# An adaLN transformer block with causal attention and a routed FFN: norms and route in pieces, value products of two units together

## The reference, cut to what matters

```python
mod = (silu(c) @ wmod).reshape(8, 6, 1, -1)      # sa, ca, ga, sb, cb, gb; |ga|, |gb| at least 0.25
h = layernorm(x) * (1 + ca) + sa
q, k, v = (lora_linear(h, ...) for 3 weights)     # x @ w.T + (x @ a.T @ b.T) / 16; 16 heads of 16
attn = softmax(where(causal, q @ k.T / 4, -inf))
x = x + ga * lora_linear(attn @ v, wo, ao, bo)
h = layernorm(x) * (1 + cb) + sb
w = top-2 of softmax(h @ Wg.T + bg), over 4 experts
base = h @ Wi.T                                   # 1024 wide
lora_e = (h @ A_e.T) @ B_e.T                      # per expert, rank 4
x = x + gb * sum_e w_e * (relu(base + lora_e) @ Wo.T)
```

## Time and profile before

| | us |
|---|---|
| median of 3 runs | 2129.84 (2129.48 to 2133.99) |
| profiled run, its own time | 2129.05 |
| its span | 2127.3 |
| TensorE busy | 1889.3 (89%), mean granted clock 0.957 |
| VectorE busy | 1219.6 (57%) |
| ScalarE busy | 943.9 (44%) |
| GpSimd busy | 489.7 (23%) |
| one full body (770.2 to 1022.8) | 252.6 |

### The profile page before, as it was taken

How to read it: one execution, slowest core, us unless ns; L and a number is a source line. 1 busy time by engine, 2 the same in 40 slices (tenths; PEclk the granted TensorE clock), 3 DMA queues, 4 the chain that set the end, 5 groups by cost and what they waited for, 6 DMA issues and landing times.

```text
span 2127.3 us, 31511 instructions
## 1 busy us (share of the span) xinstructions
PE 1889.3 (89%) x11124; PEld 978.3 (46%) x11124; DVE 1219.6 (57%) x2729; ACT 943.9 (44%) x1701; POOL 489.7 (23%) x791
## 2 busy tenths in 40 slices
PE   7699887999889997999979999799988999799858
PEld 5233443545335453454534454354533545343535
DVE  3767585555755566555665558555575555654142
ACT  2256553454444544444444444345444454444321
POOL 3122112222122312222122221222212231122213
PEclk9899998999899998999999999999989999899979
DMA  5413221212201122021211212121220112110100
GB/s 169 84 51 72 71 69 45 68 33 66 80 10 61 31 66 80 16 70 33 68 60 34 68 30 71 45 68 34 65 80 8 63 31 66 31 38 3 36 0 20
DMA packets 103024, 111.37 MB, mean 52 GB/s; under 512 B 20084, under 2 KB 96976, under 8 KB 102872
## 3 DMA queue, kind: packets, MB, share of 16 engines
q1 hardware_dynamic: 102856, 109.34, 18.1%
q10 hardware_dynamic: 16, 0.02, 0.0%
HBM read 75.20 MB, written 33.57 MB: 51 GB/s over the span
## 4 chain that ended last, share of the span: by engine, by line
PE 72%; DVE 14%; ACT 6%; issue 4%; SPq 2%; DMA 2%; POOL 1%; ACTq 0%; POOLq 0%; DVEq 0%
PE ov L768 11%; PE dense L848 11%; PE st L753 10%; PE mxs L739 10%; PE dense L859 5%; PE dense L825 5%; PE dense L783 5%; PE dense L833 4%; DVE negm L1139 3%; PE dense L724 3%; ACT probs L907 2%; PE mxs L743 2%; SPq L580 1%; PE dense L850 1%; DVE negm_left L1139 1%
## 5 line engine op out<-in xcount | busy, mean ns | idle before, releaser
L907 ACT ACTIVATE probs<-st 128x512 f32<-128x512 f32 (+1 forms) x1216 | 669.2, 575 | 653.8 <-PE st L753 644.1
L1139 DVE TENSOR_REDUCE negm<-mxs 128x1 f32<-128x384 f32 (+4 forms) x736 | 427.0, 615 | 212.7 <-PE mxs L743 209.6
L739 PE MATMUL mxs<-k_st,q_st 96*128 96x512 bf16 (+3 forms) x1536 | 469.7, 333 | 65.6 <-DVE negm L1139 59.4
L753 PE MATMUL st<-q_st,k_st 98*128 98x512 bf16 (+3 forms) x1536 | 452.8, 334 | 56.6 <-DMA q_st<-m_row 40.8
L1139 DVE TENSOR_REDUCE negm_left<-mxs 128x1 f32<-128x512 f32 x512 | 335.3, 685 | 139.8 <-PE mxs L739 138.7
L768 PE MATMUL ov<-probs,v_g 128*32 128x512 f32 (+3 forms) x3072 | 331.2, 501 | 19.5 <-POOL probs L633 18.7
L739 PEld LDWEIGHTS mxs<-k_st,q_st 96*128 96x128 bf16 x1536 | 149.4, 98 | 333.2 <-DVE negm L1139 181.6
L848 PE MATMUL dense<-c_t,wi_t 128*128 128x512 f32 x512 | 246.8, 604 | 3.9 <-ACT ratio_b L957 3.7
L753 PEld LDWEIGHTS st<-q_st,k_st 98*128 98x128 bf16 x1536 | 139.3, 99 | 240.4 <-ACT probs L907 92.4
L646 POOL TENSOR_TENSOR hid<-hid,second 128x512 f32<-128x512 f32 x128 | 159.7, 1270 | 294.1 <-DVE second L1207 293.5
L630 POOL TENSOR_TENSOR fence<-fence 128x1 f32<-128x1 f32 x256 | 49.9, 195 | 668.0 <-ACT probs L907 667.8
(11 more groups left out here) (162 smaller groups left out, 1680.8 us busy)
## 6 DMA issues: line engine op xcount, KB each, us to landing
q_st<-q_parts_scratch SPq DMA_DIRECT2D x384, 64.0 KB, 2.8
k_st<-k_parts_scratch SPq DMA_DIRECT2D x384, 64.0 KB, 2.9
q_parts_scratch<-q_part SPq DMA_DIRECT2D x16, 768.0 KB, 3.3
k_parts_scratch<-k_part SPq DMA_DIRECT2D x16, 768.0 KB, 4.9
xin<-in_L_attn_x SPq DMA_DIRECT2D x9, 1024.0 KB, 5.5
x<-in_L_attn_x SPq DMA_DIRECT2D x8, 1024.0 KB, 5.6
out_x<-ob SPq DMA_DIRECT2D x64, 128.0 KB, 1.7
q_st<-m_row SPq DMA_DIRECT2D x128, 4.0 KB
```

Source lines behind the costliest of these rows:

```text
L739: last = nc.tensor.matmul(mxs[:, bank_m, j * n:(j + 1) * n], q_st[0:KS, slot, h0 + j, qt * P:(qt + 1) * P], k_st[0:KS, slot, h0 + j, k0:k0 ...
L753: last = nc.tensor.matmul(st[:, score_bank(ch, kt, h0), j * n:(j + 1) * n], k_st[0:KS + 2, slot, h0 + j, kt * P:(kt + 1) * P], q_st[0:KS + ...
L907: nc.scalar.activation(probs[:, par, h0:h0 + heads, 0:n], st[:, score_bank(ch, kt, h0), 0:heads * n].rearrange("p (j q) -> p j q", q=n), A ...
L1139: nc.vector.tensor_reduce(dst[:, h0:h0 + heads], src, axis=AX.X, op=ALU.max, negate=True).then_inc(max_free, 1)
```

## The change

Three things, and what they need of each other.

The norms and the route are cut into pieces: two statistics a piece, the rest of a norm in seven, the route in six. `body_plan` sets them one by one between the other steps, three pieces of a norm to a unit, from unit 2 (first norm), 7 (second) and 12 (route). The instructions are the same. `t1` moves from unit 3 to 6, the projections from 4 to 7, `mt` from 14 to 15, and `ps` comes one projection later, with a wait for the four parts it writes and not for the fifth.

The value products of units 0 and 1, 2 and 3, and so on stand together after the second unit's other steps, with a third buffer of `probs`. `exp` of a unit then waits for the product three units before.

The buffer `xin` is gone. The next input is loaded at the start of a body into the half of `hid` that the FFN uses last, ahead of x1, where it was loaded a body earlier, behind `t1`; the first input goes into `ctx_n`. GpSimd, too, holds back its part of a `pj`, until after a `qk`.

```diff
+PROBS = 3
 ...
-    early.insert(4, ("ps", 0))
+    early.insert(5, ("ps", 0, 1))
 ...
-        put(3, *[("t1", i) for i in range(4)], ("xin",))
-        put(4, *early[:5])
-    if post:
-        put(9, ("ls2",), ("ln2",))
-    if pre:
-        put(11, *early[5:7])
+        put(6, *[("t1", i) for i in range(4)])
+        put(7, *early[:6])
+        put(11, *early[6:7])
     if post:
-        put(11, *[("t2", i) for i in range(4)], ("rt",), ("rx",), ("ro",))
+        put(11, *[("t2", i) for i in range(4)], ("rt",), ("rx",))
 ...
-        put(14, *[("mt", v) for v in range(2)], *[("rb", half) for half in range(2)])
+        put(15, *[("mt", v) for v in range(2)], *[("rb", half) for half in range(2)])
 ...
+    chains = []
+    if pre:
+        chains += norm_steps("1", 2)
+    if post:
+        chains += norm_steps("2", 7) + [(12 + i // 2, ("ro", i)) for i in range(ROUTE_PARTS)]
 ...
+    if pre:
+        plan.append(("xin",))
     if post:
         plan.append(("xl",))
 ...
+        beside = [s for at, s in chains if at == u]
 ...
+        turns += [((i + 0.6) / len(beside), 3, s) for i, s in enumerate(beside)]
 ...
-        plan.append(("pv", g % 2, c, kt))
+        if k % 2:
+            plan += [("pv", g % 2, *v) for v in UNITS[k - 1:k + 1]]
 ...
+POOL_IDLE = frozenset("mx pv qk nm ce ov vg ms rs t1 t2 ls1 ls2 ln1 ln2 ro ct op rt rx".split())
+STAT_PARTS = 4
+NORM_PARTS = 7
+ROUTE_PARTS = 6
+
+def norm_steps(which, first):
+    steps = [("ls" + which, i) for i in range(STAT_PARTS)] + [("ln" + which, i) for i in range(NORM_PARTS)]
+    return [(first + (i + 1) // 3, s) for i, s in enumerate(steps)]
 ...
-        xin = sb("xin", [P, T, D])
 ...
-        probs = sb("probs", [P, 2, HG, HB])
+        probs = sb("probs", [P, PROBS, HG, HB])
 ...
+        x_first = ctx_n
+        x_next = hid[:, :, :].rearrange("p a b -> p (a b)")[:, T * D:2 * T * D].rearrange("p (t d) -> p t d", t=T)
 ...
-                    sp.dma_start(xin[:, :, :], x_t[(it + 2) % NB]).then_inc(xin_in, 16)
+                    sp.dma_start(x_next, x_t[it + 1]).then_inc(xin_in, 16)
 ...
-                    ot = a[0]
-                    sp.wait_ge(part3_ready, done("pj"))
+                    ot, later = a
+                    sp.wait_ge(part3_ready, done("pj") - later)
 ...
-            walk(pool, NB, run)
+            walk(pool, NB, run, late="pj", passes=POOL_IDLE, until="qk")
 ...
-                        after(act, pv_done, done("pv"))
+                        after(act, pv_done, done("unit") - PROBS + 1)
 ...
-            def norm_stats(src, n):
+            def norm_stats(src, i):
+                for t in range(2 * i, 2 * i + 2):
+                    nc.vector.bn_stats(stats[:, t, :], src[:, t, :]).then_inc(norm_chain, 1)
 ...
-            walk(dve, NB, run, late="pj")
+            walk(dve, NB, run, late="pj", passes=("mx", "pv", "qk"), until="mx")
```

More of the change, by code:

```diff
@@ L272, in tallied @@
         names += ["scored"] * len(score_steps(*step[1:]))
+    if step[0] == "qk" and step[4] == 0:
+        names.append("unit")
     if step[0] == "qk" and step[2] == step[3] // 4 and step[4] + step[5] == HG:
         names.append("qk diagonal")
+    if step[0] in ("ln1", "ln2") and step[1] == NORM_PARTS - 1:
+        names.append("normed")
+    if step[0] in ("ls1", "ls2") and step[1] == STAT_PARTS - 1:
+        names.append(step[0] + " all")
+    if step == ("ro", ROUTE_PARTS - 1):
+        names.append("routed")
     if step[0] == "rs":
@@ L297, in with_banks, with walk @@
     return steps, n % 2
-def walk(eng, batches, run, late=None):
+def walk(eng, batches, run, late=None, passes=(), until=None):
     counts = {}
@@ L314, in done @@
                 return now.get(name, 0)
-            if held_back and s[0] not in ("mx", "pv", "qk"):
+            if held_back and s[0] not in passes:
                 run(*held_back.pop())
@@ L320, in phase @@
                 run(s, done, it, bank)
-                if held_back and s[0] == "mx":
+                if held_back and s[0] == until:
                     run(*held_back.pop())
@@ L447, in adaln_block, with normed @@
         dense = ctx.enter_context(nc.psum_tensor("dense", [P, 2, HB], F32))
+        def normed(it):
+            return x_first[:, :, :] if it < 0 else x_next
         def dense_bank(bank):
@@ L1144, in run @@
                         evacuated(dve, done)
[L1145 removed]
+                    after(dve, pv_done, done("pv") - VG_UNIT)
                     nc.vector.tensor_copy(
```

220 lines of the change are left out of this document (121 added, 99 removed).

## The result

The changed kernel takes 2152.53 us (median of 4 runs, 2151.14 to 2154.03) against 2131.91 for the kernel before: a ratio of 1.0099, 95% interval 1.0087 to 1.0111. I had forecast 2037, range 1998 to 2090. The forecast was wrong in sign.

A forecast was written before the change was run, and what follows sets the result against it. TensorE, busy nine tenths of 2127.3 us, was taken to bound the kernel. Pieces 48, pairs 30 and the end bodies 15 sum to 93 us saved, giving 2037 us, range 1998 to 2090.

The forecast's parts named there:

- part 1: Units 0 to 14 of a full body: chains in pieces save 8 us a body, 48 us in six.
- the load order and the clock: Units 0 to 14: 0.5 us for x1 behind x_next and 1 us of low clock, taken off the 9.1 us gain.
- the first and the last body: First body gains 7 us (clock, mask, row of maxima), last body 8 us; together 15, bounds 5 and 25.
- VectorE's surplus in units 2 to 5: Units 2 to 5: VectorE has 24.3 us of work, TensorE 17.5, a surplus of 6.8 us.
- the 0.5 us: At a body's first `op`: cost taken off because x1 comes behind x_next on the same queue.
- rival 4: Each body's first `op`: x_next holds VectorE 3 us, 4.5 with clock; 32 us, so 2069; with rival 1 22%.
- my worst case of 3: At a body's first `op`: VectorE stands at worst 3 us for the late x1 load.
- Part 2: Value products of two units together save 0.20 us a pair where TensorE decides; 30 us, bounds 0 and 35.
- I cost that wait at nothing: Pairs with a third buffer: `exp` waits only for the pair before, long done, so 0 us.
- my signs of being wrong: Profile after: 0.5 to 0.9 clock in units 2 to 5, VectorE waiting for x1, 0.2 us gap in pairs.
- Bodies of some 241 us: Sign of being right in the profile after: bodies of some 241 us, against 252.6.
- Rival 3: Units 2 to 5 and 8 to 14: clock stays 1.2 GHz, 23.5 us a body, 2210; 5% with the like.
- Rival 1: Pairs give nothing, the drain is paid per product: 2067, or 2101 with low bounds; with rival 4 22%.

The follow-up runs named there:

- e1: The changed kernel with x1 and the gates loaded ahead of x_next at a body's start; 2148.67 us, 1.0075 of the kernel before.
- e2: The changed kernel with value products issued one by one, not in pairs; 2138.25 us, 1.0028 of the kernel before.
- e7: e2 with x's own buffer and early load, two probability buffers, first norm's pieces in units 0 and 1; 2126.31 us, 0.9970 of the kernel before.
- e9: e7 with the first norm's pieces for the batch after next in units 33 to 35; 2089.04 us, 0.9804 of the kernel before.
- e13: e9 with each chain in one block, second norm and route where the kernel before has them; 2112.13 us, 0.9914 of the kernel before.
- e3: The changed kernel with norms and route as whole blocks at the ends of units 3, 9 and 11; 2179.54 us, 1.0214 of the kernel before.
- e4: The kernel before with an added one-megabyte load in front of x1 and the gates; 2135.12 us, 1.0011 of the kernel before.
- e5: The changed kernel with value products of units 8 and 9 single, unit 8's ahead of `nm`; 2143.29 us, 1.0054 of the kernel before.
- e11: The changed kernel with GpSimd issuing a projection's subtraction at once, not held back; 2154.54 us, 1.0102 of the kernel before.
- e6: The changed kernel with `mt`, `rb` and what follows allowed from unit 17 instead of 15; 2161.20 us, 1.0141 of the kernel before.
- e12: e9 with second norm and route moved earlier, but `t2` from unit 9 and `mt` from 15; 2094.62 us, 0.9823 of the kernel before.
- e14: e9 with second norm and route moved earlier, last two projections from unit 13, `mt` from 14; 2075.07 us, 0.9746 of the kernel before.

## Why the prediction was wrong, by its steps

**The step that failed is the sum of part 1**, "sum pair of units by pair of units and take the longer engine". Windows of the body after, by these pairs (0 and 1, 2 to 5, 6 and 7, 8 and 9, 10 and 11, 12 and 13, 14 up to `mt`):

```profile
779.35:787.79 8.44, 7.59 (x69) 4.96 (x69) 4.68 (x9) 5.67 (x11) 2.60 (x7) 1.00 0.84 233
787.79:814.76 26.97, 21.17 (x121) 11.39 (x117) 23.19 (x65) 8.35 (x14) 0.77 (x2) 0.87 0.12 38
814.76:829.00 14.24, 13.09 (x71) 6.48 (x67) 10.35 (x21) 8.48 (x15) 3.05 (x4) 1.00 0.22 56
829.00:842.44 13.44, 10.26 (x53) 4.09 (x50) 11.56 (x40) 5.01 (x9) 3.81 (x7) 0.87 0.10 41
842.44:853.73 11.29, 7.58 (x66) 4.04 (x62) 5.59 (x13) 6.45 (x11) 3.79 (x6) 1.00 0.75 164
853.73:863.85 10.12, 9.42 (x64) 4.73 (x60) 8.85 (x25) 4.82 (x10) 2.83 (x6) 1.00 0.00 0
863.85:872.30 8.45, 1.99 (x17) 0.80 (x14) 8.17 (x18) 0.60 (x1) 1.89 (x3) 0.72 0.00 1
```

| | 0, 1 | 2 to 5 | 6, 7 | 8, 9 | 10, 11 | 12, 13 | 14 to `mt` | sum |
|---|---|---|---|---|---|---|---|---|
| predicted | 8.9 | 24.3 | 13.0 | 11.2 | 9.4 | 10.1 | 5.5 | 82.4 |
| measured | 8.4 | 27.0 | 14.2 | 13.4 | 11.3 | 10.1 | 8.5 | 93.0 |

Off its sum the forecast took 1.5 us more for the load order and the clock, so it had this part at 83.9 us; the trace has 93.0, 9.1 more. (The mean of the six full bodies is within 0.2 us of this one in every column.) VectorE's work was sized nearly right, 23.2 us in units 2 to 5 for 24.3 and 11.6 in 8 and 9 for 11.2. TensorE was busy longer than I had it, 21.2 for 17.5 and 10.3 for 8.0, in part because its clock was at 0.87 in both. What failed is the rule that combines them: it has the longer engine at work from a stage's first microsecond to its last.

- Units 2 to 5, 2.7 us over. VectorE is the longer engine and has no idle time from 791.64 to 815.9, but it stood before that, for the gates (the row stands below). In e1 two other waits stand there in place of this one, and the units take 26.9 us on the mean of the six bodies against 27.1.
- Units 6 and 7, 1.2 over. TensorE was busy for 13.1 us, as foretold, and stood 1.1 for the copy of `t1` that its projection reads.
- Units 8 and 9, 2.2 over. The engines wait in turn:

```profile
836.14 0.61 PE L860 MATMUL dense<-ident_b,m_w 128*8 128x128 bf16 x8 [2.16 <-DVE m_w L1216]
...
837.58 3.29 PE L865 MATMUL dense<-h_t,w_t 128*128 128x512 f32 x4 [0.40 <-DVE rest L1224]
```

```profile
841.58 0.69 DVE L1224 TENSOR_TENSOR rest<-dense,q_part 128x512 f32<-128x512 f32 x1 [1.21 <-ACT q_part L985]
```

TensorE stands for `nm`, then does a projection in 3.29 us (1.88 at 831.88, at full clock), and VectorE stands 1.21 us for what comes of it.

- Units 10 and 11, 1.9 over: the second norm's scalings run until 846.6, and `t2` waits 1.8 us for them.
- 14 up to `mt`, 3.0 over. VectorE's work was 8.2 us for 5.5: five maxima instead of three, a projection's share of 1.06 and a copy of the route that took 1.69 here (866.44) and 1.00 before (847.05).

PE may run only three `mx` ahead, so the lead bridges none of these. Of the 115 us between forecast and result this is 9.1 x 6 = 55; the pairs are 44 (30 foretold, 14 lost) and the first and the last body 13 (15 foretold, 2 gained), which overlap a little, as the pairs cost time in the first body too. From the other end: e2 undoes the pairs, e7 beyond that the move of the first norm with its load, and with both undone the kernel is 0.3% faster than the kernel before, so these two moves carry the slowdown.

Two slips in the working are small: half the rest of a norm is 2.7 us and not 3.7 (units 8 and 9), and 0.11 of 71.8 busy us is 7.9 us of clock and not 6.7, which the sum does not use.

**The first norm.** I counted VectorE's surplus in units 2 to 5 and credited the change all the same, because the sum came out below 90.2. By the ruler its stretch lost 6.6 us a body, with the second norm's statistics now in it. e7 gives 2 of them for the old units, with a new wait; e9 gives 7.1 more a body for units in which VectorE stands, and there the norm's time does not show at all. Of e9's 42 us against the kernel before, e13 has 18 by place without any cutting. That pieces beat blocks in a given place I had right: 27 us (e3), 23 from e13 to e9. Near the old places the pieces are worth little in all: e7, with all three chains cut, is 0.3% under the kernel before.

**x_next in front of x1** (the 0.5 us, and rival 4's 4.5 us a body). VectorE stands for the gates as rival 4 said:

```profile
791.64 0.69 DVE L1248 TENSOR_TENSOR second<-dense,gates_b 128x512 f32<-128x512 f32 x1 [2.68 <-DMA gates_b<-gates_scratch]
```

That is 2.7 us, near my worst case of 3, and 12.3 us behind the body's start. Yet taking it away gave 4 us in all (e1), none of them in the full bodies, where other waits took its place; putting it into the kernel before cost 3 (e4). A wait in this list is not a price.

**Part 2, the pairs.** The local saving was sized well. The row to read beside the earlier trace rows:

```profile
1205.96 0.38 PE L793 MATMUL st<-q_st,k_st 98*128 98x512 bf16 x1
1206.27 1.92 PE L808 MATMUL ov<-probs,v_g 128*32 128x512 f32 x16
1208.12 0.39 PE L779 MATMUL mxs<-k_st,q_st 96*128 96x512 bf16 x1
```

From score to next `mx` a pair takes 2.16 us; less the score's 0.22 that is 1.94, where two single ones of the earlier trace rows take 2 x 1.08 = 2.16. 0.22 saved, as the Trainium skill's rule ("TensorEngine Tiling (Array Packing)", Key Properties) lets one expect; the trace agrees for products of 512 columns. Inside the pair the passes start 0.43 us apart all through, across the two products too. In a stretch that PE bounds, units 32 to 44, the six pairs save 0.84 us by the ruler, 0.14 each. What I left out is what a product does while VectorE finishes something: "I cost that wait at nothing" spoke of `exp` alone. The product of unit 8 was the cover of `nm`: in units 20 to 32 the pairs cost 2.2 us by the ruler (e2), as much as they save in 8 to 20 and 32 to 44 together (1.3 and 0.8). Net, the pairs were not 30 us gained but 14 lost (e2), of which e5 gives back 9; that `nm` is the whole of it is not shown.

**What was right.** No single wait of `mx` above 1.5 us in the body; pairs of 1.85 us from start to the next product (1206.27 to 1208.12); the wait for the row of maxima in the first group gone (40.8 us in the whole run before, 12.1 after; the move of `ps` was not undone by itself). The mask's wait is gone too, but not by holding GpSimd back (e11). Of my signs of being wrong two came: windows at a clock of 0.50 in units 2 to 5, and VectorE standing for what comes with x1. Bodies of some 241 us are 255.7. What came late next were `nm`, `t2` and `mt`; the sum had VectorE ahead of `mt`, and no wait for any of the three in the full bodies.

**The rivals.** Rival 3, the slower one, had the right sign, and its mechanism in part. The clock did fall in units 2 to 5, to 0.50 behind 803 to 807, where PE was busy for 1.78 of 4 us with idle pieces of 1.31 and 1.36; and again behind 867 to 871, with PE idle all through, as in the earlier trace rows. But it did not stay there, as its price supposes: it is 0.87 over units 2 to 5, and 1.00 in 10 and 11, with PE busy for 7.58 of 11.29 us. By the clock of the windows, the first part of a body lost about 10 us of TensorE's time before (0.11 of 90.2) and a whole body about 12 after (0.08 of 93.0 and 0.03 of 162.7): an estimate, of 2 us a body where the rival had 23.5. So the Trainium skill's rule of small gaps ("TensorE: Matmul & The Clock Gate", A second HAM failure mode) is not what this trace shows; behind the gap of 0.40 us before 797.54 the clock was still 1.00 (799.4 to 803.4). What the clock alone costs no run here tells, since none changes it alone. Rival 1 came true in its result (pairs give nothing), for another reason. The chance of 0.05 for slower was far too small: it rested on the clock alone, and no rival had the chain's readers waiting or a pair taking a cover away.

**The first and the last body.** 7 us gained were predicted for the first. By the ruler its units 8 to 44 take 127.5 us against 125.3 (131.60 to 259.07, and 132.81 to 258.09): `nm` waits 7.2 us in it, in 4 times, and `mx` 3.0 for the stacks that SP reads back, with the clock at 0.50 behind it (235 to 239). Nothing finer can be told: with the same steps e1 takes 124.1 us there and comes to unit 8 at 129.01 instead of 131.60. For the last body 8 were predicted, and 3.1 are gained from its unit 8 on.

## What to carry to other kernels

A chain on a second engine is free only where that engine has idle time, so list its slack unit by unit and put the chain there, even a whole stage ahead, before cutting it; moving the same norm from busy units to idle ones took 7 us off a body. Cutting then pays as well: 23 us, from blocks (e13) to pieces (e9). Do not take the longer engine per stage as its length: ask when its first input of the stage is there, and what of the stage before is still to be done. Before long matmuls are gathered, ask for each which wait of another step it covers; and do not value a wait at what the profile lists: moving `mt` away from its wait twice made the kernel slower (e6, e12), and it paid, 8 us, only with other work put in between (e14).
